# An attention stage with its exp sums moved to GpSimd and its value products moved ahead of the sums

## The reference, cut to what matters

```python
q = ln @ W_q
kv = jnp.concatenate([xn @ W_kv, ln @ W_kv], axis=1)
qn = rmsnorm(q, q_gamma) * SCALE
kn = rmsnorm(k, k_gamma)
sim = jnp.einsum('bhid,bhjd->bhij', qn, kn)
sim = jnp.where(full_mask[:, None, None, :], sim, neg)
```

## Time and profile before

| what | us |
|---|---|
| median of 3 runs | 878.85 |
| the 3 runs | 878.35, 884.24, 878.85 |
| span of the profiled execution | 875.4 |
| PE, DVE, POOL, ACT busy | 802.4, 546.3, 373.1, 366.9 |

### The profile page before, as it was taken

How to read it: one execution, slowest core, us unless ns; L and a number is a source line. 1 busy time by engine, 2 the same in 40 slices (tenths; PEclk the granted TensorE clock), 3 DMA queues, 4 the chain that set the end, 5 groups by cost and what they waited for, 6 DMA issues and landing times.

```text
span 875.4 us, 13801 instructions
## 1 busy us (share of the span) xinstructions
PE 802.4 (92%) x4270; PEld 612.4 (70%) x4271; DVE 546.3 (62%) x1173; ACT 366.9 (42%) x1175; POOL 373.1 (43%) x396
## 2 busy tenths in 40 slices
PE   6888799999999899989999999999998799999995
PEld 4555445555555555548888878888886689999994
DVE  4958765777677756675998667777766433333331
ACT  4457133544354332344444366776660032222220
POOL 7256553344447364345475044444442312222221
PEclk9999599989899988999999999999998799999998
DMA  8580000000000000003600093000001364555520
GB/s 303 170 307 35 1 0 1 1 1 0 1 1 1 0 1 1 0 1 111 255 1 0 1 301 104 12 19 13 14 12 61 101 266 176 182 180 176 174 80 3
DMA packets 31887, 67.14 MB, mean 77 GB/s; under 512 B 3103, under 2 KB 22909, under 8 KB 30813
## 3 DMA queue, kind: packets, MB, share of 16 engines
q1 hardware_dynamic: 28699, 56.17, 18.3%
q0 software_dynamic: 2560, 10.17, 3.6%
q10 hardware_dynamic: 578, 0.19, 0.1%
HBM read 54.74 MB, written 12.68 MB: 77 GB/s over the span
## 4 chain that ended last, share of the span: by engine, by line
PE 67%; DVE 17%; issue 6%; ACT 3%; POOL 3%; DMA 2%; DVEq 0%; SPq 0%; ACTq 0%; POOLq 0%
PE PS L2105 9%; PE PS L2093 9%; PE PS L1488 7%; PE PS L734 6%; PE PS L1468 6%; PE PS L1296 5%; PE PS L1274 3%; PE PS L725 3%; PE PS L771 3%; PE PS L701 3%; PE PS L726 2%; DVE row_best L846 2%; PE PS L743 2%; POOL rrms L551 2%; ACT pc L1670 1%
## 5 line engine op out<-in xcount | busy, mean ns | idle before, releaser
L1055 ACT ACTIVATE EX<-PS 128x512 f32<-128x512 f32 x144 | 78.9, 594 | 133.4 <-PE PS L726 130.6
L846 DVE TENSOR_REDUCE row_best<-PS 128x1 f32<-128x1024 f32 x64 | 77.8, 1221 | 41.8 <-PE PS L701 41.5
L1015 POOL TENSOR_TENSOR sumP<-sumP,EX 128x1024 f32<-128x1024 f32 x32 | 75.7, 2364 | 43.1 <-ACT EX L1055 42.7
L1670 ACT ACTIVATE pc<-PS,mx 128x77 f32<-128x77 f32 x256 | 78.8, 359 | 26.8 <-DVE mx L1565 26.8
L2093 PEld LDWEIGHTS PS<-xeT,w 128*128 128x128 f32 x736 | 85.6, 192 | 3.6 <-DMA w<-in_L_ffn_W 1.3
L2093 PE MATMUL PS<-xeT,w 128*128 128x128 f32 x736 | 86.1, 275 | 2.0 <-DMA w<-in_L_ffn_W 1.1
L2105 PE MATMUL PS<-w,heT 128*128 x368 | 83.3, 379 | 1.3 <-DVE oe L2035 1.3
L2132 POOL DMA_INDIRECT out<-oe,target x23 | 23.2, 1011 | 126.1 <-DVE oe L2035 126.1
L734 PE MATMUL PS<-EX,V 128*64 128x512 f32 (+1 forms) x288 | 76.5, 640 | 0.0
L2105 PEld LDWEIGHTS PS<-w,heT 128*128 128x128 f32 x368 | 68.1, 190 | 10.0 <-issue 1.7
L1488 PE MATMUL PS<-vw,pcT 128*128 128x256 f32 (+1 forms) x320 | 73.0, 383 | 1.2 <-ACT pcT L1683 1.2
(11 more groups left out here) (283 smaller groups left out, 1716.1 us busy)
## 6 DMA issues: line engine op xcount, KB each, us to landing
w<-in_L_ffn_W SPq DMA_DIRECT2D x31, 1024.0 KB, 10.1
vw_rows<-vwn SPq DMA_DIRECT2D x2, 1232.0 KB
kwH_rows<-kwH SPq DMA_DIRECT2D x1, 2464.0 KB, 7.4
kwL_rows<-kwL SPq DMA_DIRECT2D x1, 2464.0 KB, 13.7
kwH<-kwH_rows POOLq DMA_DIRECT2D x1, 2464.0 KB, 12.3
kwL<-kwL_rows POOLq DMA_DIRECT2D x1, 2464.0 KB, 19.2
vw<-vw_rows SPq DMA_DIRECT2D x2, 1152.0 KB, 13.3
XR<-in_x SPq DMA_DIRECT2D x4, 512.0 KB, 13.4
```

What stands on the lines that cost most here:

```text
L846: dve.tensor_reduce(row_best[:, n % 2, t // GT, t % GT:t % GT + 1], PSf[:, 512 * at:512 * at + S], AX.X, ALU.max, negate=True).then_inc(ma ...
L1015: pool.tensor_tensor(sumP[:], before, EX[:, (KT * n + c) % EB, :, :], ALU.add).then_inc(pool_summed, 1)
L1055: act.activation(EX[0:r, k % EB, i, :], PS[0:r, ST_AT + i, :], ACT.Exp).then_inc(exp_done, 1)
L1670: last = act.activation(pc[:, p, h * C:h * C + C], PS[:, 1 + part, (h - h0) * C:(h - h0) * C + C], ACT.Exp, bias=mx1[:, p, h:h + 1], accum ...
```

## The change

The two maxima lie side by side in one tensor `best`, and `both_max` is a reduction over it in place of an operation on two tensors. POOL adds all nine chunks (eight additions a pair) into `sumE`, with two alternating buffers; DVE's three additions a pair are gone, and `sums` waits for POOL's last. POOL takes the mean of the heads' squares (`rms2`). At step 1 PE does rows, heads, items and the value product of chunk 0 ahead of `sums`, with the order of the banks to match. DVE takes the row maximum ahead of `scale_heads`. POOL adds the bias at step 0 of pairs 3 and 4 in place of step 7, and splits the weight half behind pair 4 and half behind pair 5. The diff, cut:

```diff
+    best = sb(ctx, "best", [P, 2, 2, GT, 2])
+    sumE = att.take("sumE", [P, 2, 2, GN])
+    chunk_summed = lambda n, c: (KT - 1) * n + max(c, 1)
...
         def sums(n):
             k0 = open_bank(pe, "sum", n, 0)
-            pe.wait_ge(dve_summed, 3 * n + 3)
+            pe.wait_ge(pool_summed, chunk_summed(n, KT - 1))
...
                 if n > 0:
-                    if c == 1:
-                        sums(n - 1)
                     if c == 2:
                         project_out(n - 1, 0)
...
                     values(n, done)
+                if n > 0 and c == 1:
+                    sums(n - 1)
...
-            dve.tensor_tensor(NM[:, n % 2, i, SHIFT:SHIFT + GT], row_best[:, n % 2, i, :], ctx_best[:, n % 2, i, :],
-                              ALU.min).then_inc(shift_in, 1)
+            dve.tensor_reduce(NM[:, n % 2, i, SHIFT:SHIFT + GT], best[:, n % 2, i, :, :], AX.X, ALU.min).then_inc(shift_in, 1)
...
-            dve.tensor_scalar(rms2[:, p, 0:4], ssum[:, p, 0:4], 1.0 / E0, RMS_EPS ** 2, ALU.mult, ALU.max) \
-               .then_inc(rms_mean, 1)
...
+                if n + 1 < PP and c < 2 * GT:
+                    row_max(n + 1, c, MAX_AT)
                 for v, i in items_at(*step_before(n, c)):
                     scale_heads(v, i)
-                if n > 0 and c == 0:
-                    sum_last(n - 1)
-                if n + 1 < PP and c < 2 * GT:
-                    row_max(n + 1, c, MAX_AT)
-                if n > 0 and c == 0:
-                    sum_both(n - 1)
...
-                if c == KT - 2:
-                    sum_first(n)
...
     def pool_attend(pool):
         for n in range(PP):
-            if n > 0:
-                pool.wait_ge(dve_summed, 3 * n)
             for c in range(KT):
-                if 1 <= c < POOL_CHUNKS:
+                if n in (3, 4) and c == 0:
+                    pool_bias(pool, 1, n - 3)
+                if c == 1 and n > 1:
+                    pool.wait_ge(sum_done, n - 1)
+                if c >= 1:
+                    r = key_rows(c)
                     pool.wait_ge(exp_done, 2 * (KT * n + c) + 2)
-                    before = EX[:, KT * n % EB, :, :] if c == 1 else sumP[:]
+                    before = EX[0:r, KT * n % EB, :, :] if c == 1 else sumE[0:r, n % 2, :, :]
                     if c > 1:
-                        pool.wait_ge(pool_summed, pool_read(n, c - 1))
-                    pool.tensor_tensor(sumP[:], before, EX[:, (KT * n + c) % EB, :, :], ALU.add).then_inc(pool_summed, 1)
+                        pool.wait_ge(pool_summed, chunk_summed(n, c - 1))
+                    pool.tensor_tensor(sumE[0:r, n % 2, :, :], before, EX[0:r, (KT * n + c) % EB, :, :], ALU.add) \
+                        .then_inc(pool_summed, 1)
...
                 for v, i in items_at(n, c):
+                    pool.wait_ge(ssum_ready, unit_item(v, i) + 1)
+                    pool.tensor_scalar(rms2[:, i % 2, 0:4], ssum[:, i % 2, 0:4], 1.0 / E0, RMS_EPS ** 2, ALU.mult, ALU.max) \
+                        .then_inc(rms_mean, 1)
...
-                if n in (3, 4) and c == 7:
-                    pool_bias(pool, 1, n - 3)
...
+            if n == 4:
+                pool_wproj(pool, high=True)
             if n == 5:
-                pool_wproj(pool)
+                pool_wproj(pool, high=False)
...
-                if d < POOL_CHUNKS:
-                    act.wait_ge(pool_summed, pool_read(m, d))
-                else:
-                    act.wait_ge(dve_summed, dve_read(m, d))
+                act.wait_ge(pool_summed, chunk_summed(m, d))
```

More of the change, by code:

```diff
@@ L221, in layers_kernel @@
     EX = att.take("EX", [P, EB, 2, GN])
-    sumP = att.take("sumP", [P, 2, GN])
-    sumD = att.take("sumD", [P, 2, GN])
+    sumE = att.take("sumE", [P, 2, 2, GN])
     OT = att.take("OT", [P, 2, GN])
@@ L335, in layers_kernel @@
     (ctx_done, shift_in, rows_set, s_done, max_ready, shift_done, wq_ready, st_done, exp_done, pv_done, pool_summed,
-     dve_summed, sum_done, rl_ready, ot_ready, proj_done, proj_added) = sems(
+     sum_done, rl_ready, ot_ready, proj_done, proj_added) = sems(
          "ctx_done shift_in rows_set s_done max_ready shift_done wq_ready st_done exp_done pv_done pool_summed "
-         "dve_summed sum_done rl_ready ot_ready proj_done proj_added")
+         "sum_done rl_ready ot_ready proj_done proj_added")
     (fold_done, fold_read, fold_high, wfc_split) = sems(
@@ L620, in layers_kernel @@
     TAIL_SUM, TAIL_OUT = 1, (3, 5)
-    POOL_CHUNKS = 6
     CHUNK_OF_STEP = {1: (0,), 3: (1, 2), 5: (3, 4), 7: (5, 6), 8: (7, 8)}
@@ L625, in layers_kernel @@
     heads_of = lambda n: (2 * (n // 2 % 2), 2 * (n // 2 % 2) + 1)
-    pool_read = lambda n, c: (POOL_CHUNKS - 1) * n + max(c, 1)
-    dve_read = lambda n, c: 3 * n + (1 if c < KT - 1 else 2)
+    chunk_summed = lambda n, c: (KT - 1) * n + max(c, 1)
     FIRST_AT = {2: (0,), 4: (1,), 6: (2,), 8: (3,)}
@@ L659, in spare_uses @@
                     yield "shift", n + 1, 0
-                if n > 0 and c == 1:
-                    yield "sum", n - 1, 0
                 if n > 0 and c in (2, 4):
@@ L670, in spare_uses @@
                     yield "item", v, i
+                if n > 0 and c == 1:
+                    yield "sum", n - 1, 0
                 if n + 1 < PP and c == 8:
@@ L743, in sums @@
                     last = pe.matmul(PS[:, k0, i * GT + s:i * GT + s + 1],
-                                     sumD[:, i, s * P:s * P + P], onecol[:], start=True, stop=True)
+                                     sumE[:, n % 2, i, s * P:s * P + P], onecol[:], start=True, stop=True)
             last.then_inc(sum_done, 1)
@@ L845, in row_max @@
             dve.wait_ge(s_done, 2 * GT * n + t + 1)
-            dve.tensor_reduce(row_best[:, n % 2, t // GT, t % GT:t % GT + 1], PSf[:, 512 * at:512 * at + S],
+            dve.tensor_reduce(best[:, n % 2, t // GT, t % GT, 0:1], PSf[:, 512 * at:512 * at + S],
                               AX.X, ALU.max, negate=True).then_inc(max_ready, 1)
@@ L851, in ctx_max @@
             scores = PS[:, bank_of("ctx", n, i), 0:GT * (C + 1)].rearrange("p (s c) -> p s c", s=GT)[:, :, 0:C]
-            bank_read(dve.tensor_reduce(ctx_best[:, n % 2, i, :], scores, AX.X, ALU.max, negate=True), "ctx", n, i)
+            bank_read(dve.tensor_reduce(best[:, n % 2, i, :, 1], scores, AX.X, ALU.max, negate=True), "ctx", n, i)
         def both_max(n, i):
@@ L867, in keep_shift @@
                                         ALU.mult), "shift", n, i)
-        def sum_first(n):
-            dve.wait_ge(exp_done, 2 * (KT * n + KT - 2) + 2)
-            if n > 0:
[L872 to L884, removed]
         def reciprocals(n):
@@ L999, in dve_attend @@
                     square_sums(v, i)
-        sum_last(PP - 1)
-        sum_both(PP - 1)
         return {TAIL_SUM: lambda: reciprocals(PP - 1), TAIL_OUT[0]: lambda: add_out(PP - 1, 0),
@@ L1232, in pool_wfc, with pool_wproj @@
         pool.tensor_tensor(wfcL[:], wfc[:], wfcH[:].bitcast(F32), ALU.subtract).then_inc(wfc_split, 1)
-    def pool_wproj(pool):
-        pool.wait_ge(wfc_split, 2)
-        pool.tensor_copy(wp[:, :, 0, :], wprojT[:]).then_inc(wfc_split, 1)
+    def pool_wproj(pool, high):
+        if high:
+            pool.wait_ge(wfc_split, 2)
+            pool.tensor_copy(wp[:, :, 0, :], wprojT[:]).then_inc(wfc_split, 1)
+            return
         pool.wait_ge(wfc_split, 3)
```

4 lines of the change are left out of this document (removed).

## The result

| | before | changed |
|---|---|---|
| median, us (11 runs each) | 878.73 (875.35 to 884.29) | 869.48 (864.78 to 878.37) |
| ratio | | 0.9895, 95% interval 0.9865 to 0.9925 |
| profiled execution, span | 875.4 | 863.8 |
| attention: first key score of pair 0 to last copy of `OT` | 286.8 | 276.2 |
| time at the low clock (1.2 GHz) in the attention of the profiled execution | 34.0 | 23.8 |

The changed kernel is faster by 1.05%, 9.2 us, where 17 were forecast. The two profiled executions, 11.6 us apart, show where: 10.6 us less in the attention, 0.9 more behind it, and 1.9 less ahead of it. Ahead of the attention the change touches nothing; most of the 1.9 us comes from a fall of the clock of 3.4 us at 47.8 us that only the first execution had.

What follows compares the result with a forecast made beforehand. PE was taken to bound the attention, through its waits and low clock. Gains of 3.0, 2.0, 1.3 and 12.8 less costs of 0.4, 0.4 and 1.2 gave 17.1 us, so 862 us, range 855 to 874.

Steps and rivals of the forecast that it cites:

- rival one: Clock at pair starts: still falls at about half of them, gain 8.0 us, some 2 lost to waits; 869 us, chance 0.16.
- the signs named: Attention: no PE sum waits in pairs 1 to 7, shorter maxima, POOL near 195 us, stretch near 270, clock 0.97 or more.
- Wait for the sum: Pair starts: PE's six waits of 0.50 us for DVE's `sum_both` go, 3.0 us gained.
- Row maximum at step 0: Step 0: row maximum no longer behind `scale_heads` and `sum_last`, freeing PE's waits in pairs 2, 4 and 5; 2.0 us gained.
- Two maxima, bias earlier: `both_max` no longer held by POOL's bias additions; PE's idle 0.42 and 0.90 us go, 1.3 us gained.
- Means and powers on POOL: 18 items whose powers may stand behind POOL's additions: cost 0.4 us for all, bounds 0 to 22.
- rival three: POOL's queue heads the item chain, delaying means, powers and row maxima, 22 us lost; 894.5 us, chance 0.06.
- Mask rows: L939 ahead of the row maximum in pairs 3 and 5, held by POOL: cost 1.2 us for both.
- Rival four: DVE's remaining two-port operations held by denser additions, ten to twelve at 0.5 us each; 868 us, chance 0.07.
- Tail: Last pair: PE waits 0.2 us for POOL's last addition and POOL's first square starts late; cost 0.4 us.
- The clock: Value product ahead of `sums` shrinks the thin stretch; four of five falls go, 12.8 of 16.0 us gained.
- Rival two: Clock falls as before, from one-column matmuls or an order indifferent to idleness; only waits go; 874.5 us, chance 0.16.

Runs made afterwards that it cites:

- g4: Changed kernel with the mean of squares back on DVE and heads scaled ahead of the row maximum; 868.30 us, 0.9900 of the kernel before.
- f1: Changed kernel with the mask rows of pairs 3 and 5 written later, behind the second row maximum; 864.40 us, 0.9828 of the kernel before.
- f3: Changed kernel with both mask rows written late and `sums` 64 columns wide; 855.86 us, 0.9728 of the kernel before.
- f2: Changed kernel with the matmuls of `sums` 64 columns wide in place of one, same number and place; 863.26 us, 0.9812 of the kernel before.
- e1: Changed kernel with only the order at step 1 put back, `sums` ahead of the value product; 871.60 us, 0.9906 of the kernel before.
- g1: Changed kernel with mask rows late and `sums` 64 columns wide, but `sums` ahead of the value product; 855.16 us, 0.9729 of the kernel before.
- g3: Changed kernel with mask rows late and narrow `sums` put back ahead of the value product; 863.01 us, 0.9819 of the kernel before.
- f4: Kernel before with only the matmuls of `sums` made 64 columns wide; 870.54 us, 0.9888 of the kernel before.
- e4: Kernel before with only the order at step 1 changed, value product ahead of `sums`; 870.24 us, 0.9878 of the kernel before.

## Where the prediction was right and where it was not

The bottleneck was right: PE bounds the attention, and the time comes from its waits and its clock. 869.48 us lies inside the range of 855 to 874, but at the place of rival one (869), not of the forecast. Rival one's condition came about, falls behind four of the seven `sums`. That its number fits so well is partly luck: it gave 8.0 us to the clock and 2 to new waits, and the terms below are others.

Of the signs named, the waits, the short maxima and POOL's time came. The stretch near 270 us and the clock of 0.97 did not (276.2 and 0.94). Two signs of being wrong did: over 20 us at the low clock, and exponentials of ACT that wait for POOL, 6.9 us in three waits where before it was 2.4 in one.

```profile
ACT EX L1026 <- POOL sumE L985: 6.9, 3, 2.4
```

These waits don't reach PE, which waits 0.6 us for exponentials at L721, as it did before at L725.

- *Wait for the sum*: 3.0 predicted, 3.0 - 0.3 = 2.7 measured, the 0.3 being the tail's.
- *Row maximum at step 0*: 2.0 predicted, 2.3 measured.
- *Two maxima, bias earlier*: 1.3 predicted. Each of the 14 takes 0.16 us, as said, and PE's idle 0.42 and 0.90 in pair 5 are gone. 1.3 holds, but the move of the bias had a price elsewhere.
- *Means and powers on POOL*: 0.4 predicted; g4 shows nothing. POOL's busy time in the attention is 192 us, 195 forecast, and rival three (POOL's queue as head of the chain) did not come.
- *Mask rows*: 1.2 predicted, with at most 1.2 for each. This term was mis-sized. The bound looked at one addition of POOL, half of 2.4 us; what stands beside the write is the addition, a short cast and the four bias additions that the same change had moved there. It cost 3.2 us of waiting and a fall of 6.8 us that begins in the wait, some 6 us in all (f1 against the changed kernel; f3 against f2 gives 7). Rival four had the kind of operation right and spread it over ten places; it is one place that counts.
- *Tail*: 0.4 predicted, 0.5 measured. From the last copy of `OT` (392.3 and 379.8) to the last pair's output projection it is 6.8 us before and 7.3 us after, 0.3 of which is the wait for POOL's last addition:

```profile
399.08 1.13 PE L754 MATMUL PS<-wout,OT 64*128 64x256 f32 x8
```

```profile
387.15 1.14 PE L750 MATMUL PS<-wout,OT 64*128 64x256 f32 x8
```

From there to 664 us the two executions stay 11.8 to 12.1 us apart; the other 0.4 of the 0.9 us is lost behind that, where the clock was low for 10.2 us in the second execution and 6.8 in the first. `ffn_z` was said to end by 394.7 at the latest, within the three additions. It took 9.76 us in place of 1.39 and ended 2.5 us behind POOL's last addition (384.77 against 382.30); two further operations of POOL stand beside its end. The distance between the executions doesn't change there, so on PE it cost nothing, as said:

```profile
375.01 9.76 DVE L1344 TENSOR_SCALAR Z<-XR,mvg,rsg 128x256 f32<-128x256 f32 x4 [2.68 <-POOL rsg L1307]
...
374.87 7.43 POOL L985 TENSOR_TENSOR sumE<-sumE,EX 128x1024 f32<-128x1024 f32 x3
```

- *The clock*: this is the step that failed, "I take it that four of the five falls go". 12.8 us predicted. The profiled executions show 34.0 - 23.8 = 10.2 us less at the low clock, 10.2 x 0.47 = 4.8 us; over all executions the mean clock rises by 0.005, some 9 us of low clock or 4 us of time. The price of a low microsecond was right, and the number of falls wrong. The reason given was that the thin stretch ahead of `sums` shrinks to the 1.9 us of `sums` itself. It did shrink, and that was not enough: e1, g1 and g3 show no worth of the order here, g3 has the falls behind narrow `sums` that wait for nothing, and f2 loses them by the width alone. Rival two named the one-column matmuls as "the largest thin piece", with a chance of 0.16; its time, 874.5, was not the one measured, since some 9 us of low clock did go. Which part of the change took them is not shown. Pair 7 was one of only two pairs where the clock had held, for whatever reason; it carried 0.55 of the chance and could not.

Sum over the profiled execution's attention: 2.7 + 2.3 + 1.3 of waits, less 3.2 at the mask rows, plus 4.8 of clock, 7.9 of the 10.6 us seen. PE's idle time in the attention fell from 17.6 to 14.5 us, 3.1, which is what the waits add up to. So the 2.7 us without a line of their own are in PE's busy time, and what they are is not known.

The Trainium skill (TensorE: Matmul & The Clock Gate, Part 1, the HAM clock gate) has the clock fall after an idle window. The fall at 213.3 agrees in part: it begins in the longest wait of the attention (3.16 us), but 1.4 us into it. Those behind `sums` don't: PE is busy there, at 1.2 GHz, and the falls go away when the same sixteen matmuls of the same duration are 64 columns wide. By the rule alone f2 would have given nothing; it gave some 7 us.

## What to carry to other kernels

Price low clock from rows first, and then look for what PE did before each fall, waits and narrow matmuls both. Making narrow matmuls wider at the same duration is a cheap trial; in the old kernel it was worth as much as the whole change (f4 0.9888, changed 0.9895). When work moves to POOL, look at every DVE operation that will stand beside a *run* of POOL's work, however small it is, and take the length of the run for the bound, not that of one operation. Where there are gaps between POOL's operations, the same DVE work may slip through unheld, as `ffn_z` did in e4. Two edits that remove the same wait don't add, so try each alone before both are counted.

## What was not expected of the hardware

- Sixteen matmuls of 1 column take 1.95 us, of 64 columns 2.00 us. In the changed kernel only the first are followed by falls of the granted clock to 0.50. In the old kernel, where waits of some 0.5 us stand ahead, four of the seven wide ones are still followed by one (f4).
- A DVE `tensor_scalar` of 1x154 values from a uint8 tensor took 0.23, 0.92, 4.02 and 5.37 us, by what POOL did beside it. In the last two it was held through additions and casts that followed each other, until that run ended. The row maxima beside the same additions stayed at 1.22 us on average.
- Within one kernel the time spreads by 10 us or more from execution to execution, and the mean granted clock of the execution follows it (correlation -0.94 over 24, -0.91 over 50).
